# Row search of a mixture-of-experts kernel: second choice's slots multiplied on GpSimd, both slot tables made first

## What is computed

```python
x = x + 0.5 * ffn(layernorm(x))
x = x + attention_block(layernorm(x))
x = x + 0.5 * ffn(layernorm(x))
```

```python
logits = x @ gate_W
probs = softmax(logits)
rw, sel = top_k(probs, 2)
rw = rw / rw.sum(-1)
out = sum over the token's two experts of rw * expert(x)
```

## Time and profile before

| | us |
|---|---|
| median of 3 runs | 634.47 |
| lowest and highest of the 3 | 633.92, 644.06 |
| the profiled execution | 640.26 |
| its span (first to last instruction) | 638.5 |
| busy: TensorE, VectorE, ScalarE, GpSimd | 556.9, 457.3, 401.2, 270.7 |
| first row search: first slot table to first gather | 20.50 to 29.22 |
| second row search: first slot table to first gather | 439.78 to 447.43 |

### The profile page before, as it was taken

The page is one execution under the profiler, slowest core; times in us unless marked ns, Lnnn a source line. Parts: engine busy times, 40 slices in busy tenths (PEclk is TensorE's granted clock), DMA queues, the critical chain, the costliest instruction groups (busy, mean ns, idle before and its releaser), DMA issues. The chain is left out here.

```text
span 638.5 us, 19387 instructions
## 1 busy us (share of the span) xinstructions
PE 556.9 (87%) x6514; PEld 493.7 (77%) x6515; DVE 457.3 (72%) x1135; ACT 401.2 (63%) x954; POOL 270.7 (42%) x314
## 2 busy tenths in 40 slices
PE   9877989999999748987899988997789999999970
PEld 8867889999998634666677775676778999999960
DVE  5732867787787666499877879458467778877864
ACT  4644768898874346751265632329478789888943
POOL 7143456666644445560000005130555566666540
PEclk7567989999999878999999999997899999999996
DMA  9793122101100040000010009604111000100106
GB/s 265 229 408 114 59 70 88 37 29 33 25 17 16 18 137 2 4 4 14 3 17 4 4 19 377 282 2 133 33 35 30 27 27 26 31 29 25 29 18 201
DMA packets 41432, 46.58 MB, mean 73 GB/s; under 512 B 7408, under 2 KB 33376, under 8 KB 40352
## 3 DMA queue, kind: packets, MB, share of 16 engines
q1 hardware_dynamic: 32272, 33.99, 15.9%
q0 software_dynamic: 4736, 9.71, 5.4%
q10 hardware_dynamic: 4368, 2.10, 1.1%
HBM read 35.69 MB, written 10.09 MB: 72 GB/s over the span
## 5 line engine op out<-in xcount | busy, mean ns | idle before, releaser
L877 PE MATMUL k_y_ps<-kan_w,k_basis 128*128 x1056 | 127.3, 280 | 8.2 <-DVE k_basis L974 4.8
L877 PEld LDWEIGHTS k_y_ps<-kan_w,k_basis 128*128 128x128 f32 x1056 | 123.7, 196 | 10.1 <-issue 9.7
L867 PE MATMUL k_z_ps<-kan_w,k_basis 128*128 x528 | 120.7, 382 | 0.5 <-issue 0.5
L1140 ACT ACTIVATE k_sig<-k_h1T 128x256 f32<-128x256 f32 x264 | 84.5, 402 | 54.5 <-DVE k_h1T L999 54.3
L867 PEld LDWEIGHTS k_z_ps<-kan_w,k_basis 128*128 128x128 f32 x528 | 98.4, 191 | 13.2 <-issue 0.8
L974 DVE SCALAR_TENSOR_TENSOR k_basis<-k_sig 128x512 f32<-128x512 f32 x132 | 85.7, 690 | 15.8 <-ACT k_sig L1140 15.8
L1806 ACT ACTIVATE got<-p_ps 128x960 f32<-128x960 f32 (+1 forms) x44 | 39.3, 944 | 41.1 <-PE p_ps L1661 41.0
L1133 ACT ACTIVATE k_sig<-k_h0T 128x128 f32<-128x128 f32 x280 | 59.2, 293 | 5.9 <-DVE k_h0T L962 5.9
L693 POOL DMA_INDIRECT y_rows<-k_y,k_rows x33 | 33.6, 1019 | 48.9 <-DVE k_y L1006 31.0
L845 PE MATMUL m_z_ps<-m_xT,m_w 128*128 128x128 f32 x304 | 44.1, 292 | 9.2 <-ACT m_w L1162 7.0
L845 PEld LDWEIGHTS m_z_ps<-m_xT,m_w 128*128 128x128 f32 x304 | 42.3, 205 | 12.0 <-ACT m_w L1162 8.7
(11 more groups left out here) (270 smaller groups left out, 1063.2 us busy)
## 6 DMA issues: line engine op xcount, KB each, us to landing
kan_w<-in_L_ffn_kan_sl_W_dram SPq DMA_DIRECT2D x16, 1024.0 KB, 13.9
x_rows<-got SPq DMA_DIRECT2D x16, 256.0 KB, 2.4
mlp_w<-in_L_ffn_mlp_W_dram SPq DMA_DIRECT2D x2, 1024.0 KB, 5.8
mlp_w<-in_L_ffn_mlp_W_dram SPq DMA_DIRECT2D x8, 256.0 KB, 6.5
got<-y_rows SPq DMA_DIRECT2D x8, 256.0 KB, 4.9
got<-y_rows ACTq DMA_DIRECT2D x8, 256.0 KB, 5.4
xs<-in_L_attn_x_dram SPq DMA_DIRECT2D x4, 256.0 KB, 4.1
s_cos<-in_cos_dram SPq DMA_DIRECT2D x8, 128.0 KB
```

The source lines that it names most:

```text
L867: last = nc.tensor.matmul(z_ps, basis0[:, g], k.kan_w0[:, bass.ds(e, 1), g], start=(g == 0), stop=(g == G - 1))
L877: last = nc.tensor.matmul(y_ps, basis1[:, g, c], k.kan_w1[:, bass.ds(e, 1), c, g], start=(g == 0 and c == 0), stop=(g == G - 1 and c == F2 ...
L1140: ins = nc.scalar.activation(sig1[:, g], h1T[:], ACT.Sigmoid, bias=float(-GRID[g]))
```

## The change

In the row search VectorE makes both slot tables first, the second choice's ahead of the first's, then multiplies the first choice's table by the token numbers, then makes both row tables. The second choice's `numbers` are made by GpSimd, ahead of its first gather. TensorE's second burst waits for the new semaphore `numbers_ready` as well.

```diff
@@ route, VectorE
                 dve.wait_ge(k.const_made, k.N_CONST)
-                for j in range(TOPK):
+                for j in reversed(range(TOPK)):
                     nc.vector.tensor_tensor(in_slot[:, j], bc(slot_f[:, j], 1, NS), k.lane_of[:, 0:NS],
                                             ALU.is_equal).then_inc(in_slot_ready, 1)
-                    dve.wait_ge(in_slot_ready, j + 1)
-                    nc.vector.tensor_tensor(numbers[:, j], in_slot[:, j], bc(k.token_no[:, j], 1, NS), ALU.mult)
+                dve.wait_ge(in_slot_ready, TOPK)
+                nc.vector.tensor_tensor(numbers[:, 0], in_slot[:, 0], bc(k.token_no[:, 0], 1, NS), ALU.mult)
+                for j in range(TOPK):
                     nc.vector.tensor_tensor(in_row[:, j], bc(row_f[:, j], 1, P), k.lane_of[:],
                                             ALU.is_equal).then_inc(in_row_ready, 1)
@@ route, GpSimd
+                pool.wait_ge(in_slot_ready, 1)
+                nc.gpsimd.tensor_tensor(numbers[:, 1], in_slot[:, 1], bc(k.token_no[:, 1], 1, NS),
+                                        ALU.mult).then_inc(numbers_ready, 1)
                 pool.wait_ge(k.rows_in_dram[n], 32 * NCH)
                 pool.wait_ge(rows_ready, 1)
@@ route, TensorE
                 for j in range(TOPK):
                     pe.wait_ge(in_row_ready, j + 1)
+                    if j == 1:
+                        pe.wait_ge(numbers_ready, 1)
```

More of the change, by code:

```diff
@@ L309, in route @@
         normed, rows_ready = sem("normed"), sem("rows_ready")
-        found_ready = sem("found_ready")
+        found_ready, numbers_ready = sem("found_ready"), sem("numbers_ready")
         in_slot_ready, in_row_ready = sem("in_slot_ready"), sem("in_row_ready")
@@ L1366, in project @@
         first_added, x_ready, weighed = sem("first_added"), sem("x_ready"), sem("weighed")
-        n1_ready, nT_done, nT_ready = sem("n1_ready"), sem("nT_done"), sem("nT_ready")
-        qk_done, qk_used, v_done, v_used = sem("qk_done"), sem("qk_used"), sem("v_done"), sem("v_used")
+        n1_ready, nT_done, nT_ready = sem("n_ready"), sem("nT_done"), sem("nT_ready")
+        qk_done, qk_used, v_done, v_used = sem("products_done"), sem("products_used"), sem("rows_done"), sem("rows_used")
         rot_ready, q_spread = sem("rot_ready"), s.q_spread
@@ L1868, in finish_attention @@
         u3_ps = [ps(f"u3_ps{x}", [P, W4]) for x in range(2)]
-        wo_done, h_ready = sem("wo_done"), sem("h_ready")
+        wo_done, h_ready = sem("wo_done"), sem("rows_used")
         var_steps = sem("var_steps")
[L1871 to L1874, removed]
+        rstd_ready, n2_ready = sem("rstd_ready"), sem("n_ready")
+        nT_done, nT_ready, u_done, silu_done, hid_ready = (sem("nT_done"), sem("nT_ready"), sem("products_done"),
+                                                         sem("silu_done"), sem("products_used"))
+        y_done, h_added, x_ready = sem("rows_done"), sem("h_added"), sem("x_ready")
         stats = ChunkStats(nc, k, k.sem, "f_next")
```

## The result

| | before | after |
|---|---|---|
| median of the runs, us (20 runs each) | 637.29 | 642.73 |
| lowest and highest | 633.92, 644.06 | 636.17, 647.80 |
| profiled execution, us | 640.26 | 639.83 |
| its span | 638.5 | 638.0 |

The ratio of after to before is 1.0054, 95% interval 1.0030 to 1.0079: slower by 3.4 us, by 1.9 to 5.0, which is under 2% and counts as "the same". The median of before over 20 runs is 2.8 us higher than over the first three, so the level alone put the forecast too low; of the change, +1.5 was about half. The two profiled executions tell nothing of this: after's is 0.4 us the shorter.

A forecast was written before the change was run, and what follows sets the result against it. VectorE's row of tables was taken to bound the search up to TensorE's second burst. +1.20 in the second search and 0.3 in the first gave +1.5 us: 634.47 to 636.0 us, range 633.4 to 640.5.

The forecast's parts named there:

- VectorE's order: Row search: VectorE done 0.59 us earlier, but the first burst's table 0.48 us later; gain at the second burst 0.0 us.
- Turns between the engines: Row search: GpSimd's multiply and VectorE's tables exclude each other; second burst at 5.75 instead of 4.55, +1.20 us; chance 0.50.
- No contention: Rival: float16 tables on VectorE and GpSimd don't block each other; each search changes by 0.0, time 634.5 us; chance 0.20.
- GpSimd last: Rival: GpSimd gets no turn until VectorE's tables are done; second burst +0.77, total about +0.9, 635.4 us; chance 0.14.
- The first search: First row search: slack at gather and barrier absorbs most of the later burst; 0.3 us taken, ends 0 and 0.8.
- Everything behind the burst moves, +1.20: Second row search: gather and barrier both hang on the second burst, so the rest of the kernel moves by +1.20 us.
- The clock: Rival, second search: TensorE's longer idling brings its clock back after the barrier; 2.7 us more, 638.7 us; chance 0.13.
- shared names: 0: Projection and end of the attention: the shared semaphore names add no wait, 0 us.
- The level: Whole kernel: the forecast time was set on the runs' median of 634.47 us, giving 636.0.

The follow-up runs named there:

- m_after: The changed kernel with the loaded block counts masked with 63, against the unmasked kernel before; ratio 1.0129.
- m_after_3: The changed kernel with the loaded block counts masked with 63, a later look, against the unmasked kernel before; ratio 1.0131.
- m_after_4: The changed kernel with the loaded block counts masked with 63, one more look, against the unmasked kernel before; ratio 1.0092.
- the three bases: The kernel before with only the loaded block counts masked with 63, run three times, against it unmasked; ratios 1.0001, 1.0070 and 1.0045.
- m_before: The kernel before with only the loaded block counts masked with 63, against it unmasked; ratio 1.0001.
- extra_multiply: The kernel before, block counts masked and semaphore names shared, plus a GpSimd multiply of the first slot table into an unread tile; ratio 1.0105 to before.

## Why the prediction was right or wrong

*VectorE's order.* Right: the order alone gains nothing at the burst. 3.28 and 4.84 were measured where the same reckoning, with both multiplies on VectorE, expected 3.3 and 4.95; products run end to end are 0.1 us quicker than two bursts apart, 1.56 from start to start instead of 1.73.

*Turns between the engines.* Right in kind and size. Forecast: `numbers` ends 2.82 after the slot table, second burst 5.75. Measured: 22.52 - 19.58 = 2.94, and 5.69. The two errors are GpSimd's multiply, 0.1 us longer than the 1.5 taken, and the tighter burst. "No contention" fell with L395 at 1.88, and "GpSimd last" with it.

*The first search.* 0.3 was taken, between 0 and 0.8. In this trace, counted from the slot table, the first turned block is 15.48 - 14.67 = 0.8 later and k_xT 0.33. The first KAN product is at 36.19, and at 36.2 on average in four traces of the changed kernel (after, m_after, m_after_3, m_after_4), at 36.6 in the four of the one before (before and the three bases). So it costs nothing that shows.

*The second search: the step that failed.* "Everything behind the burst moves, +1.20" left out that TensorE itself is in the barrier with its idle products, and that they get slower: before, VectorE and TensorE arrived within 0.1 us of each other, so a move of the burst and 3.72 - 3.25 = 0.47 us more for the idle products both count. It was +1.6 at the barrier. The sum put this term at nothing without naming it.

*The clock.* Given as a rival with 0.13 and 2.7 us, with the argument that the busy stretch "moves as a whole and is no shorter". It is no shorter, but it starts later against the barrier, after 1.44 us of idling (after, m_after) or 2.35 (m_after_3, m_after_4) instead of 0.57. Since the clock came back later in all four traces than in any with an early burst, that argument did not hold: a stretch of the same length, begun later, had the clock back later. In one of the four it was late enough for the rival's case; in two the second fall was missing. Over these four the first KAN product stands 30.21 us after the slot table (28.47, 28.74, 30.68, 32.96), over the four of the kernel before at 28.29: **+1.9 us**, where the forecast had 1.2. Of m_after_4's 32.96 against the 28.6 of after and m_after, 1.65 is there at the first turned block; the rest comes after it, with the clock below full again. One trace carries much of this: without m_after_4 the mean is 29.3, +1.0. The average is at the lower end of the measured 1.9 to 5.0. The other 1.5 us to its middle is in no stage read here. Parts outside the searches vary by more than that from one execution to another (from the attention's first product of queries to the second search's slot table: 200.9 to 205.4 us in the three traces of m_before), so it stays open. The term "shared names: 0" belongs to what is open: the traces bear it out, the ratios neither do nor refute it.

*The level.* The time was given on the median of three runs, 634.47. On the median of 20 runs, 637.29, the same +1.5 gives 638.8, where the ratio gives 637.29 x 1.0054 = 640.7 and the median was 642.73. The upper end of the range, 640.5, was drawn from the same three runs and from the profiled execution, and left the spread of the runs above their median out. So the 6.7 us from 636.0 to 642.73 are 2.8 of level, 1.9 by which the ratio's +3.4 is over +1.5, and 2.0 because the median counts the long executions that the ratio leaves out.

## What to carry to other kernels

An operation moved from VectorE to GpSimd to run "beside" it can run instead of it, when both read two tensors from SBUF: here the change took 0.56 us of work off VectorE and cost it 1.32 us of standing still. A reordering that brings the producer's end forward gains nothing if the consumer needs the first part later and works without a gap from there. And where an engine idles just ahead of a barrier, count what its clock makes of the work on both sides of it.

## What the runs showed of the hardware

- A GpSimd multiply of 128x768 float16 with a repeated operand takes 1.48 us from the end of the VectorE operation that blocks it. A VectorE operation that is blocked behind it shows the wait as its own duration: 0.56 became 1.88 and 1.22 became 2.66. A fill of the same size takes 0.74 us and stretched nothing.
- GpSimd gets its turn between two VectorE instructions that stand back to back: in extra_multiply it was issued while `numbers` ran, and went ahead of `in_row`, issued 0.36 us later.
- With the same instructions in the same order (m_after, m_after_4), TensorE's clock came back 11.3 us behind the slot table in one execution and 15.7 in another, worth 1.7 us in the 16 instructions at the barrier alone (2.02 and 3.75).
